# The first scan's sums turned on VectorE, loads ahead of stores on SyncE, and the variance of x half a step later

## Chip, cores and metric

One core of one Trainium2 chip. The metric is the device time of one execution in microseconds; the kernel before was run three times.

## What is computed

x is (16, 64, 128, 64) float32: 16 images of 64 rows, 128 columns and 64 channels. Two layers are added to it in turn; _gn is a normalisation over 32 groups of two channels each.

```python
def _L0_conv_ref(x, attention_centers, attention_spreads, token_proj_n_bias):
    ...
    posmap = jax.nn.softmax(pos_score, axis=1)
    xr = x.reshape(b, w, n, v, s)
    out = jnp.einsum('mns,bwnvs->bwmvs', posmap, xr)
    out = out + token_proj_n_bias[None, :, :, :, None]
    return out.reshape(b, w, n, c)

def _L1_conv_ref(x, W):
    rows = jnp.moveaxis(x, 1, 0)
    row0 = rows[0]
    def step(carry, row):
        new = row + jax.nn.relu(conv1d_same(carry, W))
        return (new, new)
    _, outs = jax.lax.scan(step, row0, rows[1:])
    out = jnp.concatenate([row0[None], outs], axis=0)
    return jnp.moveaxis(out, 0, 1)

x = x + _L0_conv_ref(_gn(x), ...)
x = x + _L1_conv_ref(_gn(x), L1_conv_W)
```

The first layer mixes each image's columns with four 128x128 matrices (one per head). The second runs down the 64 rows of an image: each new row is the normalised row plus the rectified convolution (9 taps along the columns, 64 by 64 channels) of the row before. That scan is sequential in the rows and independent between images.

## The kernel before

The 16 images go in two waves of eight. A setup phase (to about 180 us) prepares the first eight images. Then the first scan (wave 0) runs its 64 steps over these eight images, and beside it the other eight images are prepared, one per iteration of eight steps. A boundary follows, and then the second scan (wave 1) of 64 steps, with nothing beside it.

A step works in two halves s = 0, 1 of four images each. Data of the scan lie with (two columns' channels) on the 128 partitions and 256 elements (64 column pairs of four images) along each. For each half, in this order of dependence:

- PE, `convolve` (L1033): 15 matmuls into ps_conv; ten need carry_h (the high part of the row before, L1037) and the last five carry_l (its rest, L1041).
- VectorE, carry (L825): the rectified convolution plus the normalised row.
- ScalarE, carry_h (L543), rounded from carry; then VectorE, carry_l (L835), carry less carry_h.
- GpSimd, `add_carry` (L410): total, which is x after the first layer plus carry: a row of the output, still with the columns of an image scattered.

**From total to the output.** In wave 0, PE's `turn_out` (L1022) transposes total of both halves by four 128x128 matmuls against the identity into ps_out, right behind the step's first convolution; ScalarE's `stage_out` (L517) copies ps_out into one of two buffers `staged`; SyncE's `store_row` (L295) stores it with two DMAs of 128 KB in runs of 512 bytes. In wave 1, VectorE's `flip_out` (L804) transposes total in blocks of 32x32 straight into `staged`, behind the next step's carry of the same half; the rest of the turning is in the addresses of eight DMAs of 32 KB in runs of 128 bytes (`flipped_block`, L237), of which SyncE issues five (L306) and ScalarE three (L525). A buffer may be written again when its stores of two rows before have landed; GpSimd may write total again when it has been turned.

**Beside wave 0.** Each engine's `prep` function puts the next image's work into the steps by hand. The letter i is the step in an iteration, and VectorE counts four gaps in a step: gap 0 between carry and carry_l of half 0, gap 1 behind that carry_l, gaps 2 and 3 the same for half 1. Per iteration:

- GpSimd scales x by the first normalisation in eight halves of a quarter (`scale_half`, L379); PE mixes one in each step (`mix_half`, L949), at the end of the step; VectorE adds that to x in steps 1, 3, 5, 7, gap 3 (`mix_to_x1`, L732); PE turns it in steps 0, 2, 4, 6 (`turn_in`, L962); ScalarE keeps it (`keep_in`, L491) and normalises rows for the scan (L513).
- Statistics of the image after that (x of b + 1): 16 bn_stats on VectorE (L638), two or three each in gaps 0, 1, 2 of step 3, gaps 0, 2 of step 4 and gaps 0, 1 of step 5; PE averages them over the partitions at the end of step 5 (mean1, L965); VectorE's dev (step 5, gap 3), ScalarE's dev2 (end of step 5); PE's var1 (step 6, behind the first convolution, L969); ScalarE's root std1 (step 6, half 0); VectorE's guess1 (step 6, gap 2); ScalarE's square1 (end of step 6); VectorE's ratio1 and rstd1 (step 7, gap 0) and mean_rstd1 (step 7, gap 2); PE's shift1 (end of step 7, L974).
- Loads: SyncE issues four loads of 512 KB per iteration, in steps 1, 3, 5, 7, each behind that step's stores (L324 to L327). A load waits until PE has turned the quarter that the buffer held.

Each engine executes its own instructions in the order written; semaphores are the only links between engines.

## Time and profile before

| | us |
|---|---|
| runs | 787.57, 787.59, 785.27 (median 787.57) |
| profiled execution, its own time | 787.0 |
| its span | 785.2 |
| setup and first eight images | to about 183 |
| first scan | about 183 to 535 |
| boundary | about 535 to 552 |
| second scan | to the end |

Over the span PE is busy 703.5 us (90%), VectorE 580.8 (74%), ScalarE 524.2 (67%), GpSimd 421.0 (54%). Such a share is an average over stages with different limits; the page's strip of 40 slices shows PE at nine tenths or more in nearly every slice of both scans. How to read the rows further below: a row of a timeline is start, duration, engine, line, operation and tiles, with merged neighbours as "x2", and in brackets the idle time of that engine before it and what ended it. PE's weight loads (PEld) run beside its matmuls, whose recorded durations overlap, so the time that a piece of PE's work takes is read from start to start.

### The profile page before, as it was taken

Reading aid. Unit: us, or ns where it says so; the run is one execution under the profiler, and the core shown is the slowest. Engines: PE = TensorE matmul, PEld = TensorE weight load, DVE = VectorE, ACT = ScalarE, POOL = GpSimd, SP = SyncE. Lnnn points to the kernel's source line nnn. Section 1 sums busy time; section 2 is a strip of 40 time slices with the busy share of each in tenths; the row PEclk is TensorE's granted clock in tenths of the full one; section 3 lists DMA queues with packets and bytes.
Section 4 is the critical chain, followed back from the end, with each engine's and each line's share of the span. In section 5 each row is a group of like instructions: output and inputs, shape, how many; then the busy total and the mean of one; then the engine's idle time right before and its main releaser. Section 6 shows DMA issues by size and latency. Waiting matters only on the chain.

```text
span 785.2 us, 18039 instructions
## 1 busy us (share of the span) xinstructions
PE 703.5 (90%) x5356; PEld 671.4 (86%) x5356; DVE 580.8 (74%) x1298; ACT 524.2 (67%) x918; POOL 421.0 (54%) x416
## 2 busy tenths in 40 slices
PE   1577777767999999999999999995999999999996
PEld 1466666667999999999999999995999999999996
DVE  7589999955868787786868777664766767777775
ACT  1167767785877777777777777756566666666661
POOL 1555566623655556565656565661455555555553
PEclk9889999998999999999999999998999999999999
DMA  9846556132434443444434431221344444444444
GB/s 179 157 109 133 122 121 134 28 81 49 100 76 101 108 95 84 94 108 94 93 81 107 96 80 43 53 56 27 52 74 76 71 73 74 71 75 68 78 69 80
DMA packets 307594, 68.11 MB, mean 87 GB/s; under 512 B 274772, under 2 KB 307540, under 8 KB 307540
## 3 DMA queue, kind: packets, MB, share of 16 engines
q1 hardware_dynamic: 255316, 61.15, 38.0%
q10 hardware_dynamic: 52224, 6.30, 5.2%
q8 instruction: 26, 0.43, 0.2%
q14 instruction: 28, 0.23, 0.1%
HBM read 33.85 MB, written 33.55 MB: 86 GB/s over the span
## 4 chain that ended last, share of the span: by engine, by line
PE 58%; DVE 15%; issue 11%; ACT 7%; ACTq 6%; POOL 1%; SPq 0%; DVEq 0%; DMA 0%; POOLq 0%
PE ps_conv L1037 26%; PE ps_conv L1041 13%; PE ps_mix L949 9%; PE ps_in L962 6%; ACTq L533 5%; DVE st L638 5%; PE ps_out L1029 3%; ACT x_paired L491 2%; DVE carry L825 2%; ACT carry_h L543 2%; PE ps_small L939 2%; DVE x_sb L732 2%; DVE st L739 2%; ACT rows L513 1%; DVE rows L732 1%
## 5 line engine op out<-in xcount | busy, mean ns | idle before, releaser
L410 POOL TENSOR_TENSOR total<-x_paired,carry 128x256 f32<-128x256 f32 x256 | 234.2, 915 | 256.6 <-DVE carry L825 145.8
L835 DVE TENSOR_TENSOR carry_l<-carry,carry_h 128x256 fp32r<-128x256 f32 x252 | 166.1, 659 | 82.6 <-ACT carry_h L543 74.1
L543 ACT ACTIVATE carry_h<-carry 128x256 fp32r<-128x256 f32 x252 | 105.5, 419 | 162.9 <-DVE carry L825 115.8
L513 ACT ACTIVATE rows<-x_paired,shift,rstd 128x256 f32 (+1 forms) x256 | 213.4, 842 | 0.2
L1037 PE MATMUL ps_conv<-carry_h,wh 128*128 128x256 f32 x1280 | 208.1, 293 | 4.7 <-ACT carry_h L543 4.2
L491 ACT ACTIVATE x_paired<-ps_in,shift 64x512 f32<-64x512 f32 (+1 forms) x256 | 174.8, 683 | 30.2 <-PE ps_in L962 26.0
L1041 PE MATMUL ps_conv<-carry_l,wh 128*128 128x256 f32 x1280 | 194.6, 282 | 0.0
L1037 PE MATMUL ps_conv<-carry_h,wl 128*128 128x256 f32 x1280 | 193.9, 282 | 0.0
L1037 PEld LDWEIGHTS ps_conv<-carry_h,wh 128*128 128x128 f32 x1280 | 170.6, 191 | 8.1 <-ACT carry_h L543 6.9
L379 POOL TENSOR_TENSOR xs<-x_sb,minus_rstd 128x512 f32<-128x512 f32 x104 | 147.9, 1435 | 43.8 <-DVE minus_rstd L714 40.9
L1037 PEld LDWEIGHTS ps_conv<-carry_h,wl 128*128 128x128 f32 x1280 | 171.0, 189 | 0.0
L1041 PEld LDWEIGHTS ps_conv<-carry_l,wh 128*128 128x128 f32 x1280 | 171.0, 189 | 0.0
L825 DVE SCALAR_TENSOR_TENSOR carry<-ps_conv,rows 128x256 f32<-128x256 f32 x256 | 106.6, 417 | 72.9 <-PE ps_conv L1041 62.7
L949 PE MATMUL ps_mix<-xs,mix 128*128 128x256 f32 x384 | 102.2, 397 | 0.0
L739 DVE BATCH_NORM_STATS2 st<-x_paired 128x6 f32<-128x512 f32 (+1 forms) x128 | 85.4, 681 | 8.9 <-ACT x_paired L491 8.9
L949 PEld LDWEIGHTS ps_mix<-xs,mix 128*128 128x128 f32 x384 | 70.6, 199 | 7.2
L638 DVE BATCH_NORM_STATS2 st<-x_sb 128x6 f32<-128x256 f32 x208 | 75.0, 412 | 0.0
L962 PE MATMUL ps_in<-ident,x_sb 128*128 128x128 f32 x416 | 55.4, 277 | 15.5 <-ACT x_paired L491 11.3
L962 PEld LDWEIGHTS ps_in<-ident,x_sb 128*128 128x128 f32 x416 | 48.0, 143 | 22.7 <-issue 19.0
L812 DVE STREAM_TRANSPOSE staged<-total 128x256 f32<-128x256 f32 x128 | 55.4, 433 | 3.6 <-DMA out_dram<-staged 3.4
L732 DVE SCALAR_TENSOR_TENSOR x_sb<-ps_mix,bias_col,x_sb 128x1024 f32<-128x1024 f32 x42 | 53.5, 1274 | 3.2 <-PE ps_mix L949 3.2
L379 POOL TENSOR_TENSOR xs<-rows,minus_rstd 128x512 f32<-128x512 f32 x24 | 31.3, 1334 | 32.7 <-DVE minus_rstd L714 31.2
(92 smaller groups left out, 396.7 us busy)
## 6 DMA issues: line engine op xcount, KB each, us to landing
x_sb<-in_x_dram SPq DMA_DIRECT2D x52, 512.0 KB, 4.2
out_dram<-staged SPq DMA_DIRECT2D x128, 128.0 KB, 2.4
out_dram<-staged SPq DMA_DIRECT2D x320, 32.0 KB, 1.6
rows<-in_x_dram SPq DMA_DIRECT2D x12, 512.0 KB, 4.1
out_dram<-staged ACTq DMA_DIRECT2D x192, 32.0 KB, 1.7
x_paired<-in_L_conv_W_dram SPq DMA_DIRECT2D x2, 80.0 KB, 2.7
x_paired<-in_L_conv_W_dram SPq DMA_DIRECT2D x2, 64.0 KB, 2.5
x_paired<-v_attention_centers_dram SPq DMA_DIRECT2D x1, 0.0 KB
```

Of the source, the lines that this page charges most:

```text
L379: nc.gpsimd.tensor_tensor(xs[:, c % 2, heads, :, :].rearrange("p s h v -> p h v s"), src, minus_rstd1[:, k, m:G:2].unsqueeze(1).unsqueeze( ...
L410: nc.gpsimd.tensor_tensor(total[s][:, :].rearrange("p (w j) -> p w j", w=WS), x1_rows(wave, it, i, 1, s * WS, WS)[:, 0, :, :], carry[s][:, ...
L491: ins = nc.scalar.activation(dst[q * C:(q + 1) * C, r:CR:2, :], src[:, q, :, :], ACT.Identity, bias=shift1[r * C:(r + 1) * C, k:k + 1])
L513: nc.scalar.activation(rows[:, g % 2, :, w // WS, :, w % WS], x1_rows(wave, it, g * RG, RG, w, 1)[:, :, 0, :], ACT.Identity, scale=rstd2[: ...
L543: nc.scalar.activation(carry_h[s][:, EDGE:EDGE + J, :].rearrange("p j w -> p (j w)"), carry[s][:, :], ACT.Copy).then_inc(high_ready[s], 1)
L638: ins = nc.vector.bn_stats(st1[:, 0, 2 * m:2 * m + 2, :].rearrange("p g k -> p (g k)"), v[:, m, :, :, :])
L825: nc.vector.scalar_tensor_tensor(carry[s][:, :], ps_conv[:, s * BANK:s * BANK + SW], 0.0, rows[:, (i // RG) % 2, i % RG, s, :, :].rearrang ...
L835: nc.vector.tensor_tensor(carry_l[s][:, EDGE:EDGE + J, :].rearrange("p j w -> p (j w)"), carry[s][:, :], carry_h[s][:, EDGE:EDGE + J, :].r ...
L949: ins = nc.tensor.matmul(ps[:, s * CR * V:(s + 1) * CR * V], mix[:, s, :], xs[:, c % 2, s, :, :].rearrange("p h v -> p (h v)"), start=True ...
L962: ins = nc.tensor.transpose(ps_in[:, k * P:(k + 1) * P], x_bufs[e][:, at:at + P], ident[:, :])
L1037: nc.tensor.matmul(ps_conv[:, s * BANK:s * BANK + SW], w[:, d, :], carry_h[s][:, d:d + J, :].rearrange("p j w -> p (j w)"), start=(w is wh ...
L1041: ins = nc.tensor.matmul(ps_conv[:, s * BANK:s * BANK + SW], wh[:, d, :], carry_l[s][:, d:d + J, :].rearrange("p j w -> p (j w)"), start=F ...
```

## The change

VectorE's flips, so far in the second scan alone, now turn the first scan's sums too: `flip_out` runs behind carry in both waves, and twice more behind the last step of wave 0. `turn_out`, `stage_out` and `store_row` are gone, with ps_out's use for rows. GpSimd's add waits for the flip of its half. SyncE stores each row of wave 0 with eight DMAs of 32 KB, all on its own queue (in wave 1 still five, with three on ScalarE's), and in each step it now issues the load, if there is one, ahead of the row's stores. The variance of x is worked out half a step later: PE's var1 behind the mix of step 6 in place of behind its first convolution, ScalarE's std1 in half 1 of step 6 and square1 in half 0 of step 7, VectorE's guess1 in gap 0 of step 7 and ratio1 and rstd1 in gap 2, ahead of mean_rstd1.

```diff
@@ sync
             def store_flipped(wave, h, buf):
-                rows_flipped = held(sp, h + 1)
+                rows_flipped = held(sp, wave * H + h + 1)
                 alone(sp, w_zeroed)
                 for s in range(NS):
                     sp.wait_ge(out_flipped[s], rows_flipped)
-                for block in range(SP_BLOCKS):
+                for block in range(BLOCKS if wave == 0 else SP_BLOCKS):
                     dst, src = flipped_block(wave, h, buf, block)
                     sp.dma_start(dst, src).then_inc(flip_stored[buf], 16)
...
-                    if wave == 1 and not (is_zero(it) and i == 0):
-                        store_flipped(wave, it * STEPS + i - 1, (i + 1) % 2)
-                    if wave == 0 and not (is_zero(it) and i == 0):
-                        store_row(wave, it * STEPS + i - 1, (it + wave * ITERS) * STEPS + i, (i + 1) % 2)
                     if i == 1 and more >= 1:
                         load_chunk(b + 1, 1 - e, CH - 1, CH * b)
                     if i in (3, 5, 7) and more >= 2:
                         load_chunk(b + 2, e, (i - 3) // 2, CH * b + (i - 3) // 2 + 1)
+                    if not (is_zero(it) and i == 0):
+                        store_flipped(wave, it * STEPS + i - 1, (i + 1) % 2)
@@ gpsimd, add_carry
-                if wave == 0 and not is_zero(t):
-                    pool.wait_ge(out_turned, t)
...
+                if not is_zero(t):
+                    pool.wait_ge(out_flipped[s], t)
@@ scalar, iteration
-                        if s == 0 and wave == 0 and not begins:
-                            stage_out(t, (i + 1) % 2)
...
-                        if s == 0 and i == 6 and more:
+                        if s == 1 and i == 6 and more:
                             std1_of(b + 1)
+                        if s == 0 and i == 7 and more:
+                            square1_of(b + 1)
...
-                    if i == 6 and more:
-                        square1_of(b + 1)
@@ vector, prep
-                    if i == 6 and gap == 2:
+                    if i == 7 and gap == 0:
                         guess1_of(b + 1)
-                    if i == 7 and gap == 0:
+                    if i == 7 and gap == 2:
                         ratio1_of(b + 1)
                         rstd1_of(b + 1, 1 - e)
-                    if i == 7 and gap == 2:
                         mean_rstd1(b + 1, 1 - e)
@@ vector, flip_out
-                if isinstance(h, int) and h < 2:
-                    dve.wait_ge(stored[buf], H // 2 * 32)
-                else:
-                    dve.wait_ge(flip_stored[buf], 128 * (it * (STEPS // 2) + (i - 1) // 2))
+                if not (wave == 0 and isinstance(h, int) and h < 2):
+                    dve.wait_ge(flip_stored[buf], 128 * (wave * H // 2 + it * (STEPS // 2) + (i - 1) // 2))
@@ vector, iteration, and behind the last step of wave 0
-                        if wave == 1 and not (is_zero(it) and i == 0):
+                        if not (is_zero(it) and i == 0):
                             flip_out(wave, it, i, s)
...
+            for s in range(NS):
+                dve.wait_ge(total_ready[s], H)
+                flip_out(0, ITERS, 0, s)
             finish(B - 1, 1)
@@ tensor, prep and iteration
-                if after == 0:
-                    if i == 6 and more:
-                        var1_of(b + 1, inv_p[:, :], 1)
-                else:
+                if after == 1:
                     mix_half(b, i // 2, i % 2, ps_mix, b * CH + i // 2)
                     if i == 0 and prev:
                         turn_in(b - 1, 1 - e, CH - 1)
+                    if i == 6 and more:
+                        var1_of(b + 1, inv_p[:, :], 1)
...
-                            if s == 0 and wave == 0:
-                                turn_out(t)
```

## Rows read from the trace of the kernel before

**Rows 1.** Busy us (instructions) by engine in a stretch; then granted clock, DMA share, GB/s.

```profile
core 0: us, PE busy (x) PEld busy (x) DVE busy (x) ACT busy (x) POOL busy (x), PEclk, DMA share, GB/s
302.00:346.00 44.00, 43.78 (x348) 42.29 (x347) 34.08 (x69) 33.82 (x61) 25.75 (x26) 1.00 0.42 95
```

**Rows 2.** Chain of waits, 300 to 560: start us, duration us, what.

```profile
343.93 0.74 DVE st L638 x2
...
433.15 0.74 DVE st L638 x2
```

**Rows 3.** Timeline, PE: transposes between convolutions, and convolutions of the second scan.

```profile
353.72 0.60 PE L1029 MATMUL ps_out<-ident,total 128*128 128x128 f32 x4
354.08 0.83 PE L1037 MATMUL ps_conv<-carry_h,wh 128*128 128x256 f32 x5
...
355.92 1.03 PE L949 MATMUL ps_mix<-xs,mix 128*128 128x256 f32 x4
...
603.05 0.75 PE L1037 MATMUL ps_conv<-carry_h,wh 128*128 128x256 f32 x5
...
604.82 0.75 PE L1037 MATMUL ps_conv<-carry_h,wh 128*128 128x256 f32 x5
```

**Rows 4.** Timeline of a half step of the second scan; the flip's line (min/median/max ns).

```profile
601.47 0.42 DVE L825 SCALAR_TENSOR_TENSOR carry<-ps_conv,rows 128x256 f32<-128x256 f32 x1
...
601.81 0.43 DVE L812 STREAM_TRANSPOSE staged<-total 128x256 f32<-128x256 f32 x1
...
602.38 0.43 DVE L835 TENSOR_TENSOR carry_l<-carry,carry_h 128x256 fp32r<-128x256 f32 x1
...
602.48 1.05 POOL L410 TENSOR_TENSOR total<-x_paired,carry 128x256 f32<-128x256 f32 x1 [0.18 <-DVE staged L812]
...
L812 DVE STREAM_TRANSPOSE staged<-total x128: 427/433/448, 552.5 to 779.5; 128x256 f32<-128x256 f32 x128
```

**Rows 5.** Groups by line, VectorE, 302 to 346 and 560 to 780: busy, mean | idle before.

```profile
L835 DVE TENSOR_TENSOR carry_l<-carry,carry_h 128x256 fp32r<-128x256 f32 x16 | 12.6, 787 | 4.5 <-ACT carry_h L543 4.5
...
L835 DVE TENSOR_TENSOR carry_l<-carry,carry_h 128x256 fp32r<-128x256 f32 x120 | 67.5, 563 | 43.1 <-ACT carry_h L543 35.0
```

**Rows 6.** Timeline of steps 3 to 5: first carry, VectorE's idle time, PE's mean1.

```profile
330.98 0.42 DVE L825 SCALAR_TENSOR_TENSOR carry<-ps_conv,rows 128x256 f32<-128x256 f32 x1 [0.43 <-PE ps_conv L1041]
...
342.21 0.42 DVE L825 SCALAR_TENSOR_TENSOR carry<-ps_conv,rows 128x256 f32<-128x256 f32 x1 [1.19 <-PE ps_conv L1041]
...
345.09 0.31 PE L939 MATMUL ps_small<-st,inv_p 128*128 128x32 f32 x2
```

**Rows 7.** Timeline: POOL's add begun before carry_l.

```profile
345.17 0.87 POOL L410 TENSOR_TENSOR total<-x_paired,carry 128x256 f32<-128x256 f32 x1 [1.45 <-DVE carry L825]
...
345.48 0.84 DVE L835 TENSOR_TENSOR carry_l<-carry,carry_h 128x256 fp32r<-128x256 f32 x1 [0.48 <-ACT carry_h L543]
```

**Rows 8.** Timeline: var1 on PE; ratio, rstd, product with the mean; shift1 on PE.

```profile
347.90 0.30 PEld L939 LDWEIGHTS ps_small<-st,inv_p 128*128 128x128 f32 x2 [0.45 <-ACT dev L454]
...
354.26 0.19 DVE L707 SCALAR_TENSOR_TENSOR ps_small<-ps_small,square 128x32 f32<-128x32 f32 x1
354.57 0.19 DVE L714 SCALAR_TENSOR_TENSOR minus_rstd<-ps_small,guess 128x32 f32<-128x32 f32 x1
...
356.46 0.28 DVE L719 TENSOR_TENSOR minus_mean_rstd<-ps_small,minus_rstd 128x128 f32<-128x128 f32 x1
...
356.80 0.30 PEld L939 LDWEIGHTS ps_small<-col_avg,minus_mean_rstd 128*128 128x128 f32 x2 [0.25 <-DVE minus_mean_rstd L719]
```

**Rows 9.** Timeline, ScalarE at the boundary: the last copy from ps_out.

```profile
539.37 0.60 ACT L523 ACTIVATE staged<-ps_out 128x512 f32<-128x512 f32 x1
```

**Rows 10.** Stores on SyncE's queue (ns to issue), and DMA issues (KB, us to landing).

```profile
L314 SPq DMA_DIRECT2D out_dram<-staged x320: 315/316/2336, 555.2 to 783.1; - x160
...
L303 SPq DMA_DIRECT2D out_dram<-staged x128: 595/607/1723, 189.4 to 540.7; - x128
...
x_sb<-in_x_dram SPq DMA_DIRECT2D x52, 512.0 KB, 4.2
...
out_dram<-staged SPq DMA_DIRECT2D x320, 32.0 KB, 1.6
```

More of the change, by code:

```diff
@@ L200, in mix_and_scan_kernel @@
         total_ready = [sem(f"total_ready{s}") for s in range(NS)]
-        out_turned = sem("out_turned")
-        out_staged = sem("out_staged")
-        stored = [sem(f"stored{n}") for n in range(2)]
         out_flipped = [sem(f"out_flipped{s}") for s in range(NS)]
@@ L293, in _ @@
                 load_chunk(W + 1, 1, c, CH * (W - 1) + c + 1)
-            def store_row(wave, h, t, buf):
-                staged_rows = held(sp, t)
-                alone(sp, w_zeroed)
-                sp.wait_ge(out_staged, staged_rows)
-                src = staged[:, buf, :].rearrange("p (m f) -> p m f", f=P)
-                for e in range(2):
-                    dst = out_pairs[wave * W + e:(wave + 1) * W:2, bass.ds(h, 1), :, :]
-                    sp.dma_start(dst.rearrange("m h j f -> (h j) m f"),
-                                 src[e * J:(e + 1) * J, :, :]).then_inc(stored[buf], 16)
             def store_flipped(wave, h, buf):
-                rows_flipped = held(sp, h + 1)
+                rows_flipped = held(sp, wave * H + h + 1)
                 alone(sp, w_zeroed)
@@ L557, in iteration @@
                     if wave == 1 and not begins:
-                        store_flipped(1, it * STEPS + i - 1, (i + 1) % 2)
+                        store_flipped(wave, it * STEPS + i - 1, (i + 1) % 2)
                     if b is not None:
@@ L828, in iteration @@
                             ALU.max, ALU.add).then_inc(carry_ready[s], 1)
-                        if wave == 1 and not (is_zero(it) and i == 0):
+                        if not (is_zero(it) and i == 0):
                             flip_out(wave, it, i, s)
@@ L1020, in finish @@
                 var2_of(b, wave)
-            def turn_out(t):
-                if not (isinstance(t, int) and t <= 1):
-                    pe.wait_ge(out_staged, t - 1)
-                for s in range(NS):
-                    pe.wait_ge(total_ready[s], t)
-                    for m in range(WS // 2):
-                        ins = nc.tensor.transpose(ps_out[:, s * SW + m * P:s * SW + (m + 1) * P],
-                                                  total[s][:, m * P:(m + 1) * P], ident[:, :])
-                ins.then_inc(out_turned, 1)
             def convolve(t, s):
```

18 lines of the change are left out of this document (3 added, 15 removed).

## The prediction

> **What bounds the kernel now.** I read the busy times by stretch first, then the chain of waits through the same stretch, then the timeline of one iteration. One iteration of the first scan (eight steps, one image prepared beside them) takes 44.6 us (343.93 to 433.15, two of them [rows 2]); the stretch 302 to 346 is nearly all of one, and in it PE is busy 43.78 of 44.00 us, VectorE 34.08, ScalarE 33.82 and POOL 25.75, with the granted clock at 1.00, so at the higher of its two levels, 2.4 GHz [rows 1]. What leaves PE's queue here is time gained, until something else ends last. The chain names the candidate: although PE is so full, the chain leaves it once per iteration, in step 5, for VectorE's statistics of x [rows 2]. VectorE is close to being the bound in a few steps long before it is one on average.
>
> **What leaves PE.** In every step but the first, four transposes stand between the step's two convolutions. They start at 353.72, the next convolution at 354.08 (0.36 us), and that convolution takes 1.84 us to the mix behind it; in the second scan, where a convolution follows another directly, it takes 1.77 (603.05 to 604.82) [rows 3]. So the transposes cost 0.36 + 0.07 = 0.43 us. 63 steps have them: 27.1 us less, 3.4 us per iteration. The 64th set, after the last step, lies beside VectorE's last mix_to_x1, which the turning of the image waits for: nothing. ScalarE loses 64 copies of 0.60 us; it has idle time in every step, so only the one at the scans' boundary counts, where it stands ahead of seven row normalisations in a row that ScalarE does back to back [rows 9]: 0.6 us less.
>
> **What VectorE gains in work.** 126 transposes move from the nearest row's form, the flips of the second scan: 0.433 us each, hardly varying [rows 4]. There carry lasts 0.42 but the flip starts 0.34 after it, so an instruction gives way some 0.08 before its recorded end; I take 0.35 per flip. In most half steps this is free: carry_l waits for ScalarE's carry_h anyway and starts 0.91 after carry with the flip in between (601.47 to 602.38) [rows 4], and before, the wait in that place was 4.5 us in this stretch [rows 5].
>
> It isn't free in steps 3 to 5, where bn_stats fill the gaps. PE's average of these statistics (mean1, in step 5, 7 iterations) stands behind the last of them. Before, counted from carry of step 3 at 330.98: the last pair of statistics begins at 343.93 and ends at 344.67 [rows 2], so 13.69 us, of which VectorE idled 1.19 (ahead of 342.21); PE came for them at 345.09, 14.11 us after the same start, so nothing waited [rows 6]. After: VectorE runs without idling, 13.69 - 1.19 + 5 flips x 0.35 = 14.25, with 0.06 to reach PE 14.31 (0.06 as from 356.74, the end of minus_mean_rstd, to 356.80 [rows 8]). PE is there after 14.11 - 3 x 0.43 = 12.82. PE waits 1.5 us: 10.5 us over 7 iterations. Later mixes and convolutions that would have waited for a late VectorE (carry_h, or POOL's scaled halves behind the later adds) have these 1.5 us too, so I add nothing for them.
>
> Bounds: carry_l lasts 0.84 where POOL's add began first (345.17 against 345.48) and 0.43 where carry_l did (602.38 against 602.48) [rows 4, 7]. If the three long ones of this run become short, 3 x 0.41 = 1.2 less: 0.3 us wait. If the flips take all of 0.433 (+0.4) and two more carry_l become long (+0.8): 2.7. I take 1.5, since statistics still stand ahead of carry_l in those steps and the add, 0.67 behind the flip's start, gets ahead of it.
>
> **POOL.** Its add waited for carry and for PE's transposes; now it waits for the flip, and starts 0.67 after the flip's start [rows 4], so about a flip later than carry alone would let it. Behind the add stand the next add and a scaled half for the coming mix. POOL is busy 25.75 of 44.00 us [rows 1], so 0.4 us later is covered except where VectorE is already late, and there mean1 is waited for longer.
>
> **The variance, half a step later.** Six instructions move: PE's var1 behind the mix, ScalarE's root and square, VectorE's guess, ratio and rstd. Gained: PE's wait for ScalarE's dev in front of var1, 0.45 us in 7 iterations [rows 8]; the mix, recorded with 1.03 [rows 3], now covers it: 3.1 us. Lost: ratio, rstd and the product with the mean now all stand in the last half step, behind carry and flip, and PE's shift1 waits for the product. Before, the product stood right behind carry, so 0.34 after its start, and PE waited 0.25 for it (356.80). After: 0.34 + flip 0.35 + ratio to rstd 0.31 (354.26, 354.57) + 0.31 of the same kind = 1.31, so 0.97 later, all of it PE's wait, since PE already waited: 6.8 us [rows 8]. Bounds: 0.6 if the flip's wait is shared, 1.4 if a long carry_l precedes it. On ScalarE the root waits in a later place with keep_in and the next carry_h behind it, a step of slack; POOL's first scaled half waits for rstd no longer than for its own add.
>
> **SyncE's queue.** Eight stores of 32 KB for two of 128 KB: 0.316 to issue each, landing 1.6 later [rows 10], so 8 x 0.32 = 2.5 us of a 5.3 us step, with a load on odd steps. The load now waits for in_turned ahead of the eight stores; that comes from PE in the step before, and the stores wait for flips of this step, so the wait is over first. The flip two rows on waits for the stores: 8.4 us after the row's last flip (below), against 2.5 + 1.6. Behind a flip that waits stand carry_l, the gap's work and the next carry, so PE would follow. I take nothing. Bounds: no gain, since nothing waited for stores before; a loss only under the last rival.
>
> **Sum.** Against the profiled execution's 787.0 (span 785.2 and 1.8 around it; median of runs 787.57, so 0.6 higher): -27.1 + 10.5 + 6.8 - 3.1 - 0.6 = -13.5, so 773.5. With the lower bounds of both waits, -27.1 + 2.1 + 4.2 - 3.1 - 0.6 = -24.5: 762.5. With the upper ones, -27.1 + 18.9 + 9.8 - 3.1 - 0.6 = -2.1: 785.
>
> **Rivals.** (1) VectorE fits: short carry_l almost everywhere, both waits near their lower bounds, 763. For it: the second scan's order, carry, flip, carry_l, is now the first's. Against: there no statistics stand in the gaps.
>
> (2) Both waits near the upper bounds: 785, hardly a gain.
>
> (3) Slower: VectorE bounds the whole wave. Its place is carry_l behind POOL's add in every half step, which the flip starts: add 0.67 after the flip's start, 0.87 long, carry_l's end 0.28 after that (345.17 + 0.87 to 345.48 + 0.84) [rows 4, 7]. A half step then takes 0.34 + 1.82 - 0.08 = 2.08, sixteen 33.3; of VectorE's other work, 34.1 less carry (16 x 0.34) and carry_l (16 x 0.71, its mean of 0.79 less 0.08 [rows 5]) = 17.3, the 16 statistics (0.66 a pair, 5.3) fit into that wait, so 45.3, and 0.6 for ratio and rstd: 45.9 against 44.6. Over 7 iterations 9.1 more: 796. It decides from the point where carry_h comes later than the add, 0.67 after the flip. For it: in the second scan carry_l wins by 0.10 only (602.38 against 602.48). Against it: it does win there mostly, with a mean of 0.563 [rows 5], and the scan isn't bound by it. By the Trainium skill ("VectorE: DVE Perf Modes", Rules for kernel authors) 128x128 transposes belong on TensorE where PSUM will do, the 32x32 ones on VectorE; by the first half of it this move costs. No row shows it as a rule: here TensorE is the full engine.
>
> (4) The stores land late: if each took 0.607 to issue, as the 128 KB one [rows 10], behind a load of 4.2 us, 4.9 + 4.2 + 1.6 = 10.7 us pass the 8.4 that two buffers give (two steps of 5.3 less a convolution and a flip), 2.3 us on 4 rows of each iteration, 74 us in all: near 847. It decides from 0.32 each with the load right ahead. Against it: the same store took 0.316 (median of 320), and SyncE issues the load once the row before is out, 5.3 - 2.5 us ahead of the flips. The Trainium skill ("DMA: Bandwidth & Descriptors", Specifications) wants 512 B per transfer, below which it expects read-modify-write; these write 128 B runs, and the second scan, which does too, lets VectorE run on.
>
> **How the numbers follow.** Forecast 0.53, (1) 0.15, (2) 0.17, (3) 0.12, (4) 0.03. The range 762 to 786 holds the first three. 0.3% is 2.4 us, about what a measurement tells from no change; faster takes the forecast, (1) and 0.10 of (2): 0.78; same 0.07 of (2); slower (3) and (4): 0.15.
>
> **What would show it.** In the profile after: PE without L1029; a first-scan iteration of 43.2 us (44.6 - 3.4 + 1.5 + 0.97 - 0.45); PE idle ahead of mean1 on VectorE's statistics, 1.5 us, 7 times, and ahead of shift1 on minus_mean_rstd, 1.2 us; none ahead of var1; flips at 0.43 with no wait for stores. Wrong if the two waits aren't there (then nearer 763), if convolutions wait for carry_h or carry_l in steps 0 to 2 (then 796), or if flips wait for stores.

## The result, and the profile of the kernel after

The kernel after takes 775.16 us (median; 774.53 to 779.17), the kernel before 786.42 in the same comparison: a ratio of 0.9867, 95% interval 0.983 to 0.990. So it is 11.3 us faster where 13.5 were forecast, and 775.2 lies 1.7 above the forecast of 773.5. The profiled execution of the kernel after took 779.17, with a span of 777.4; it is the slowest of them.

The page's line of busy times after, over the whole span:

```profile
PE 682.4 (88%) x5100; PEld 645.6 (83%) x5100; DVE 592.8 (76%) x1426; ACT 490.2 (63%) x854; POOL 431.0 (55%) x416
```

PE works 21 us less than before (703.5), ScalarE 34 less (524.2). VectorE works 12 more (580.8), though its new flips take 55. The groups of carry_l in the first scan tell why (busy, mean | idle before), after and before:

```profile
L799 DVE TENSOR_TENSOR carry_l<-carry,carry_h 128x256 fp32r<-128x256 f32 x124 | 63.8, 514 | 10.9 <-ACT carry_h L513 2.2
```

```profile
L835 DVE TENSOR_TENSOR carry_l<-carry,carry_h 128x256 fp32r<-128x256 f32 x123 | 92.1, 749 | 36.5 <-ACT carry_h L543 36.4
```

The flip fills VectorE's wait for carry_h, 36.5 us that are down to 10.9, and since GpSimd's add now starts behind the flip, carry_l mostly starts ahead of the add (31 of 126 take over 0.65 us, 109 before) and is 28 us shorter in all: so most of the flips' time is paid for in the place where they stand.

Where the span got shorter is to be seen in the time from one carry to another. The first carry of every iteration of eight steps stands in the timeline, here of iterations 5 and 6:

```profile
356.21 0.42 DVE L789 SCALAR_TENSOR_TENSOR carry<-ps_conv,rows 128x256 f32<-128x256 f32 x1 [0.97 <-PE ps_conv L996]
...
401.23 0.42 DVE L789 SCALAR_TENSOR_TENSOR carry<-ps_conv,rows 128x256 f32<-128x256 f32 x1 [0.60 <-PE ps_conv L996]
```

Their differences, in both kernels, are the seven iterations with an image prepared beside them:

| first-scan iteration | 1 | 2 | 3 | 4 | 5 | 6 | 7 | sum |
|---|---|---|---|---|---|---|---|---|
| before, us | 42.55 | 44.57 | 44.50 | 44.72 | 44.51 | 44.34 | 44.40 | 309.6 |
| after, us | 41.78 | 42.68 | 42.93 | 43.28 | 45.02 | 42.83 | 42.56 | 301.1 |

The forecast was 43.2 for each. Iterations 2, 3, 6 and 7 are a little better than that, iteration 4 is at it, and iteration 5 is 1.8 us worse and even longer than before. The ledger of the two profiled executions, from the same carries:

| stretch | before | after | difference |
|---|---|---|---|
| start to the first carry of the first scan | 183.2 | 185.5 | +2.3 |
| seven iterations | 309.6 | 301.1 | -8.5 |
| eighth iteration and the boundary | 54.8 | 50.2 | -4.6 |
| second scan, first to last carry | 230.0 | 233.0 | +2.9 |
| behind the last carry | 7.6 | 7.6 | 0 |

The two lines of the first scan hold the change's own work: -13.1 for -13.5 forecast. The setup has no changed instruction, and its end moves from one profiled execution to the next (181.0 in the fastest kernel below, 183.3 in another). The granted clock up to there moves with it: 0.94 here, 0.96 before, 0.98 and 0.96 in those two. So +2.3 belongs to this execution; without it the ledger gives -10.2, near the 11.3 of the medians. The +2.9 of the second scan was not forecast.

The two waits that the prediction put a price on are both there. The waits of the first scan after (us in total, times, longest):

```profile
PEld ps_small L906 <- DVE minus_mean_rstd L686: 7.5, 7, 1.1
PE ps_small L906 <- DVE st L605: 7.3, 7, 1.1
PEld ps_small L906 <- DVE st L605: 7.2, 5, 1.5
DVE staged L776 <- DMA out_dram<-staged: 3.4, 2, 1.8
PEld ps_small L906 <- issue: 2.9, 2, 1.4
```

and the same view of before:

```profile
PEld ps_small L939 <- ACT dev L454: 2.9, 7, 0.5
PEld ps_small L939 <- DVE minus_mean_rstd L719: 1.8, 7, 0.3
```

PE's weight load is what waits first, so its rows carry the price. For mean1 (on VectorE's statistics, st) it waits 7.2 us in five iterations, and in the other two the same wait of 1.4 is put down to "issue", with the matmul behind it still naming st: 10.1 us in seven, for 10.5 forecast. For shift1 (on minus_mean_rstd) it waits 7.5 for 1.8 before: 5.7 more, for 6.8. The wait ahead of var1 (on dev), 2.9 before, is gone, for 3.1. One row was forecast not to be there: flips wait for their buffer's stores, 3.4 us.

The chain of mean1, from the timeline of steps 4 to 6 of one iteration:

```profile
416.04 0.42 DVE L789 SCALAR_TENSOR_TENSOR carry<-ps_conv,rows 128x256 f32<-128x256 f32 x1 [1.02 <-PE ps_conv L996]
...
417.05 0.87 POOL L388 TENSOR_TENSOR total<-x_paired,carry 128x256 f32<-128x256 f32 x1 [1.09 <-DVE staged L776]
417.36 0.84 DVE L799 TENSOR_TENSOR carry_l<-carry,carry_h 128x256 fp32r<-128x256 f32 x1
...
429.66 0.74 DVE L605 BATCH_NORM_STATS2 st<-x_sb 128x6 f32<-128x256 f32 x2
430.46 0.30 PEld L906 LDWEIGHTS ps_small<-st,inv_p 128*128 128x128 f32 x2 [1.47 <-DVE st L605]
```

From carry of step 3 to PE's mean1 it is 430.46 - 416.04 = 14.42, for 14.31 forecast, and PE's wait is 1.47 for 1.5. The add at 417.05 starts ahead of carry_l at 417.36, which then takes 0.84: the long carry_l that the prediction left in these steps, 0.28 past the add's end.

The chain of shift1, in the last half step of an iteration:

```profile
351.90 0.42 DVE L789 SCALAR_TENSOR_TENSOR carry<-ps_conv,rows 128x256 f32<-128x256 f32 x1 [0.44 <-PE ps_conv L996]
352.25 0.43 DVE L776 STREAM_TRANSPOSE staged<-total 128x256 f32<-128x256 f32 x1
352.60 0.17 DVE L674 SCALAR_TENSOR_TENSOR ps_small<-ps_small,square 128x32 f32<-128x32 f32 x1
352.89 0.19 DVE L681 SCALAR_TENSOR_TENSOR minus_rstd<-ps_small,guess 128x32 f32<-128x32 f32 x1
353.12 0.29 DVE L686 TENSOR_TENSOR minus_mean_rstd<-ps_small,minus_rstd 128x128 f32<-128x128 f32 x1
353.46 0.30 PEld L906 LDWEIGHTS ps_small<-col_avg,minus_mean_rstd 128*128 128x128 f32 x2 [1.14 <-DVE minus_mean_rstd L686]
```

The product starts 1.22 after carry, for 1.31 forecast (rstd to product took 0.23, not 0.31), and PE waits 1.14. One flip costs VectorE 0.35 here (352.25 to 352.60), as taken.

### What the long steps of iteration 5 wait for

SyncE's queue holds the answer. Its stores and loads around them, from the timeline (merged neighbours as x16; the lengths of a merged row hold the gaps between its stores):

```profile
343.01 2.75 SPq L299 DMA_DIRECT2D out_dram<-staged  x1
...
358.65 0.81 SPq L299 DMA_DIRECT2D out_dram<-staged  x2
...
362.64 0.89 SPq L299 DMA_DIRECT2D out_dram<-staged  x2
...
366.87 0.42 SPq L267 DMA_DIRECT2D x_sb<-in_x_dram  x1
367.61 8.72 SPq L299 DMA_DIRECT2D out_dram<-staged  x16
```

and the whole line of the stores, with what SyncE does between two of them (min/median/max ns):

```profile
L299 SPq DMA_DIRECT2D out_dram<-staged x832: 315/316/2752, 193.0 to 775.3; - x167
L299 SPq FUSED_REGOPS  x536: 37/37/66, 272.7 to 772.7; - x179
```

A store is still recorded with 0.316 here, but stores follow each other at 0.50 us (two at 358.65 take 0.81 = 0.50 + 0.31), so that eight are 4.0 us, not 2.5. From 272.7 on the program runs in a loop and works its addresses out in registers, and a register operation and a move stand between two stores; they don't make the pace, though. Ahead of the loop and behind it nothing stands between two stores of a row, one from the second on is recorded with 0.45, and the next begins 0.49 after its start. A row of eight takes as long in the loop (first line) as behind it (second):

```profile
283.12 3.81 SPq L299 DMA_DIRECT2D out_dram<-staged  x8
...
504.24 3.78 SPq L299 DMA_DIRECT2D out_dram<-staged  x8
```

The kernel before had this pace too, in the five stores of a row of its second scan (2.31 = 4 x 0.50 + 0.31):

```profile
613.74 2.31 SPq L314 DMA_DIRECT2D out_dram<-staged  x5
```

The first store right behind a load takes longer, 0.7 to 1.2 us in twelve of thirteen places (1.09 at 367.61) and 2.75 in the other; 14 of the first scan's other 499 stores took 0.8 to 1.7 as well. And at the loop's end SyncE issues nothing from 359.46 to 362.64: 0.12 behind the last store stands its jump, 2.74 us pass from that to the next instruction, and the flips of the row that it goes on with had ended at 358.82. The same jump takes 0.33 in the kernel before and 0.19 in the run without flips (below), where a pass of SyncE's loop has 170 and 42 instructions; in every run whose pass has 362 or 458 it takes 2.5 to 2.8, in one 3.7. An estimate from these rows: 16 rows at 4.15, 8 loads at 1.4 with what the store behind them loses, and the jump make 80 us of the 86 that 16 steps of 5.35 have. The queue is all but full.

The flips that waited, both of them in iteration 5 (VectorE):

```profile
367.73 0.45 DVE L776 STREAM_TRANSPOSE staged<-total 128x256 f32<-128x256 f32 x1 [1.59 <-DMA out_dram<-staged]
...
373.45 0.45 DVE L776 STREAM_TRANSPOSE staged<-total 128x256 f32<-128x256 f32 x1 [1.77 <-DMA out_dram<-staged]
```

The row issued from 362.64 on goes out until 366.5 and has landed at 367.7, where the first flip starts. The next row is issued from 367.61, behind a load, with a first store of 1.09, and lands at about 373.4. Had the first row been issued 2.7 us earlier, as its flips allowed, it would have landed at about 365.0, ahead of 366.14, where VectorE came for the buffer, and the next one at about 370.7, ahead of 371.68. But the jump alone doesn't do it: SyncE came to it late. The store of 2.75 us at 343.01 had put it behind, and the last row ahead of the jump went out from 354.86, 2.2 us after its flips (352.68). In the run with the variance back (below), whose queue is the same, SyncE issued that row 0.2 after its flips; its jump took 2.54, the next row went out 1.7 after its flips, no flip waited, and iteration 5 took 43.71, the one before it 43.95. So in this execution the long store, the jump and the pace of 0.50 together made the two waits, and the steps of 5.60 and 7.95 us (5.27 and 6.15 in the iteration before). No run took the jump away, and why it takes 2.74 no row shows.

### The profile page after: what moved, and what is told of

Read it like the earlier page. It is cut to its first block, busy times and chain, and to the rows that moved or that the text cites. A ratio compares the mean times of both kernels' runs of the same rounds, so it can differ in the third digit from the quotient of the medians.

```text
span 777.4 us, 18263 instructions
## 1 busy us (share of the span) xinstructions
PE 682.4 (88%) x5100; PEld 645.6 (83%) x5100; DVE 592.8 (76%) x1426; ACT 490.2 (63%) x854; POOL 431.0 (55%) x416
## 4 chain that ended last, share of the span: by engine, by line
PE 46%; DVE 23%; issue 13%; ACTq 6%; ACT 6%; SPq 3%; POOL 1%; DVEq 1%; DMA 0%; POOLq 0%
PE ps_conv L992 22%; PE ps_conv L996 11%; DVE st L605 7%; PE ps_mix L916 7%; ACTq L503 6%; PE ps_in L929 5%; DVE carry L789 3%; DVE st L706 3%; SPq L299 3%; DVE carry_l L799 2%; ACT carry_h L513 2%; DVE staged L776 2%; PE ps_small L906 2%; ACT x_paired L469 2%; DVE x_sb L699 2%
## 5 line engine op out<-in xcount | busy, mean ns | idle before, releaser
L388 POOL TENSOR_TENSOR total<-x_paired,carry 128x256 f32<-128x256 f32 x256 | 252.2, 985 | 237.8 <-DVE staged L776 230.6
L992 PE MATMUL ps_conv<-carry_h,wh 128*128 128x256 f32 x1280 | 204.7, 291 | 6.7 <-ACT carry_h L513 6.3
L799 DVE TENSOR_TENSOR carry_l<-carry,carry_h 128x256 fp32r<-128x256 f32 x252 | 134.6, 534 | 58.9 <-ACT carry_h L513 41.9
L361 POOL TENSOR_TENSOR xs<-x_sb,minus_rstd 128x512 f32<-128x512 f32 x104 | 139.8, 1356 | 45.7 <-DVE minus_rstd L681 34.1
L776 DVE STREAM_TRANSPOSE staged<-total 128x256 f32<-128x256 f32 x256 | 110.7, 433 | 5.4 <-DMA out_dram<-staged 5.0
L916 PE MATMUL ps_mix<-xs,mix 128*128 128x256 f32 x384 | 105.3, 407 | 0.6 <-DVE x_sb L699 0.4
```

The lines of the kernel that those rows point to most:

```text
L361: nc.gpsimd.tensor_tensor(xs[:, c % 2, heads, :, :].rearrange("p s h v -> p h v s"), src, minus_rstd1[:, k, m:G:2].unsqueeze(1).unsqueeze( ...
L388: nc.gpsimd.tensor_tensor(total[s][:, :].rearrange("p (w j) -> p w j", w=WS), x1_rows(wave, it, i, 1, s * WS, WS)[:, 0, :, :], carry[s][:, ...
L776: nc.vector.transpose(staged[:, buf, s * SW:(s + 1) * SW], total[s][:, :]).then_inc(out_flipped[s], 1)
L799: nc.vector.tensor_tensor(carry_l[s][:, EDGE:EDGE + J, :].rearrange("p j w -> p (j w)"), carry[s][:, :], carry_h[s][:, EDGE:EDGE + J, :].r ...
L916: ins = nc.tensor.matmul(ps[:, s * CR * V:(s + 1) * CR * V], mix[:, s, :], xs[:, c % 2, s, :, :].rearrange("p h v -> p (h v)"), start=True ...
L992: nc.tensor.matmul(ps_conv[:, s * BANK:s * BANK + SW], w[:, d, :], carry_h[s][:, d:d + J, :].rearrange("p j w -> p (j w)"), start=(w is wh ...
```

## Experiments

Each run stands against the kernel before on the same chip (787 to 788 us). Line numbers in rows are those of the kernel that ran. First, the transposes alone.

**No flips in the first scan**

```diff
-                if not (is_zero(it) and i == 0):
+                if wave == 1 and not (is_zero(it) and i == 0):
                     flip_out(wave, it, i, s)
...
             def store_flipped(wave, h, buf):
+                if wave == 0:
+                    return
```

(The waits that count flips and stores change with it.)

> The changed kernel without the first scan's turning and without its stores, but for the last row's flip (the first eight images are not written). Theory A (PE's transposes cost 0.43 us each, and VectorE's flips give 1.5 us per iteration back in PE's wait for mean1): an iteration of 44.6 - 3.4 - 0.45 + 0.6 = 41.3 us, no wait ahead of mean1, 786.4 - 27.1 - 3.1 + 4.3 - 0.6 = 760 us. Rival R1 (the transposes cost PE less than that, and nothing is given back): the iteration stays at the changed kernel's 42.7 and the time near 774.

Measured: 760.48 us, ratio 0.967 (0.964 to 0.970); iterations 2 to 7 of 40.9 to 41.4 us, 41.3 expected. What the transposes on PE cost is thereby gained in full where nothing takes their place, and the 15 us between this run and the kernel after are what the flips and their stores give back. The waits of its first scan:

```profile
PEld ps_small L908 <- DVE minus_mean_rstd L688: 5.2, 7, 0.8
```

mean1's wait is down to 1.3 us in five iterations; shift1's falls to 5.2 but stays, since the moved ratio and rstd make it too.

**Four statistics fewer, so that the last ones end in step 4** (the last four of 16 are left out)

```diff
-                    if i == 5 and gap < 2:
-                        stats1(b + 1, 1 - e, 12 + 2 * gap, 2)
```

> The changed kernel without the four statistics instructions of step 5 (two gaps of two; their groups keep the image before's values). Theory A (PE's mean1 waits for VectorE's run from step 3 to the last statistics): the run is 4 x 0.33 = 1.3 us shorter and ends a carry_l earlier, PE waits for nothing there, 1.4 us less per iteration, 7 iterations, 775.2 - 10 = 765. Rival R2 (what waits next is nearly as late: the mix waits for GpSimd's scaled half behind the flips, or a convolution for carry_h): 2 us less, 773, with PE's wait moved there.

Measured: 766.62 us, ratio 0.976 (0.972 to 0.980); iterations 40.81, 41.40, 41.57, 42.47, 43.74, 41.47, 41.25. The waits of its first scan:

```profile
PEld ps_small L904 <- DVE minus_mean_rstd L686: 7.5, 7, 1.1
DVE staged L774 <- DMA out_dram<-staged: 5.1, 6, 1.7
```

PE no longer waits for statistics, and the time falls by 8.5, near the 10.1 of that wait. The rest went to the buffers: flips wait 5.1 us for stores, 3.4 in the kernel after. A PE that comes round sooner meets the same store queue.

**The same with all the work in it: statistics from step 2 on.** Gap 3 of step 2 takes three of them, and step 5 keeps one.

```diff
+                    if i == 2 and gap == 3:
+                        stats1(b + 1, 1 - e, 0, 3)
...
-                        stats1(b + 1, 1 - e, 2 * gap, 2)
+                        stats1(b + 1, 1 - e, 3 + 2 * gap, 2)
...
-                        stats1(b + 1, 1 - e, 6 + 3 * gap // 2, 3)
-                    if i == 5 and gap < 2:
-                        stats1(b + 1, 1 - e, 12 + 2 * gap, 2)
+                        stats1(b + 1, 1 - e, 9 + 3 * gap // 2, 3)
+                    if i == 5 and gap == 0:
+                        stats1(b + 1, 1 - e, 15, 1)
```

> The changed kernel with its 16 statistics begun earlier: three at the end of step 2, where VectorE idles 1.0 us, six in step 3, six in step 4, one in step 5. Nothing is left out. Theory A: VectorE's run from step 3 to the last statistics is 3 x 0.33 + the carry_l and two statistics behind it shorter, 12.6 against PE's 12.8, no wait ahead of mean1: 1.4 us less per iteration, 775.2 - 10 = 765.5. Rival R2 (the work only moves, and the next late thing is nearly as late): 773.

Measured: 768.19 us, ratio 0.977 (0.975 to 0.980), 2.7 above the expectation; iterations 41.02, 41.47, 43.08, 42.57, 43.92, 41.50, 41.26. Outside iterations 3 to 5 they are those of the run before. In 3 to 5 flips wait:

```profile
DVE staged L778 <- DMA out_dram<-staged: 7.0, 8, 1.8
```

**The variance moved back, the flips kept**

```diff
@@ scalar, iteration
-                        if s == 1 and i == 6 and more:
+                        if s == 0 and i == 6 and more:
                             std1_of(b + 1)
-                        if s == 0 and i == 7 and more:
-                            square1_of(b + 1)
...
+                    if i == 6 and more:
+                        square1_of(b + 1)
@@ vector, prep
+                    if i == 6 and gap == 2:
+                        guess1_of(b + 1)
                     if i == 7 and gap == 0:
-                        guess1_of(b + 1)
-                    if i == 7 and gap == 2:
                         ratio1_of(b + 1)
                         rstd1_of(b + 1, 1 - e)
+                    if i == 7 and gap == 2:
                         mean_rstd1(b + 1, 1 - e)
@@ tensor, prep
-                if after == 1:
+                if after == 0:
+                    if i == 6 and more:
+                        var1_of(b + 1, inv_p[:, :], 1)
+                else:
...
-                    if i == 6 and more:
-                        var1_of(b + 1, inv_p[:, :], 1)
```

> The changed kernel with the variance of x in its old places. Theory A (the move pays together with the flips): VectorE's dev and ScalarE's dev2 come some 1.0 us after PE has reached the old place of var1, so PE waits about 1.1 there; ahead of shift1 it waits 0.6 less. 0.5 more per iteration, 775.2 + 3.5 = 779. Rival R3 (the move only adds a wait, ahead of shift1): 0.5 less per iteration, 772.

**The variance moved alone, in the kernel before** (the same lines the other way)

> The kernel before with the variance's move alone. Theory A: var1's wait of 0.45 goes, the product comes 0.6 later behind ratio and rstd and PE waits for it: 0.2 more per iteration, 786.4 + 1 = 787.5, not told from no change. Rival R5 (the move is worth something by itself): 0.45 less per iteration with the product's delay covered, 783.

Measured: moved back 779.78 us, ratio 0.992 (0.990 to 0.995), so 4.6 slower than the kernel after. Moved alone 785.24, ratio 0.998 (0.997 to 1.000): a gain of 1.3 us by the ratio, 2.6 at most by its interval, between the two expectations, and its iterations are those of before (44.58, 44.42, 44.74, 44.42 in the middle). The rows that tell why, first with the variance back:

```profile
PEld ps_small L907 <- ACT dev L432: 7.8, 7, 1.1
...
PEld ps_small L907 <- DVE minus_mean_rstd L686: 5.1, 7, 1.0
```

then with it moved alone:

```profile
PEld ps_small L938 <- DVE minus_mean_rstd L719: 5.2, 7, 0.8
```

Without flips the move takes var1's wait away (2.9) and raises shift1's from 1.8 to 5.2: nothing is left of it. With flips var1's wait would have been 7.8 and shift1's 5.1 in any case; the move trades 7.8 for 2.4. So it pays only together with the flips. In an iteration of the run with the variance back, var1 waits for ScalarE's part of dev:

```profile
433.24 0.23 ACT L432 ACTIVATE dev<-dev 128x32 f32<-128x32 f32 x1
```

VectorE's part was done at 431.63, but ScalarE was at its keep_in (431.83 to 433.21), which stands behind a carry_h that VectorE's run of statistics and flips had made late. It starts 2.9 us after PE's mean1, 2.5 in the kernel before, and PE, with no transposes between, comes to var1 2.0 after mean1, 2.4 before.

**Ratio and rstd out of shift1's chain.** In step 7 guess1 (half 0) and the product (half 1) go ahead of the flip, ratio and rstd into the gap between, and ScalarE's square1 ahead of its row normalisation.

```diff
@@ scalar, iteration
+                        if s == 0 and i == 7 and more:
+                            square1_of(b + 1)
...
-                        if s == 0 and i == 7 and more:
-                            square1_of(b + 1)
@@ vector, iteration
+                        if b is not None and more and i == 7:
+                            if s == 0:
+                                guess1_of(b + 1)
+                            else:
+                                mean_rstd1(b + 1, 1 - e)
                         if not (is_zero(it) and i == 0):
                             flip_out(wave, it, i, s)
@@ vector, prep
-                    if i == 7 and gap == 0:
-                        guess1_of(b + 1)
-                    if i == 7 and gap == 2:
+                    if i == 7 and gap == 1:
                         ratio1_of(b + 1)
                         rstd1_of(b + 1, 1 - e)
-                        mean_rstd1(b + 1, 1 - e)
```

> The changed kernel with the variance's last links shortened: in step 7 guess and the product with the mean stand ahead of the flip, ratio and rstd one gap earlier, ScalarE's square ahead of its row normalisation. Theory A: the product begins 0.34 after carry in place of 1.22, PE's wait ahead of shift1 falls from 1.1 to 0.25, 0.85 less per iteration, 775.2 - 6 = 769. Rival R6 (PE then waits for something else there, carry_l or the mix): 774.

Measured: 770.95 us, ratio 0.980 (0.978 to 0.982); 769 expected of a wait that bounds, 774 of one that is hidden. The wait is back at the value of before, and 4.2 us of its 5.7 show up in the time (6.1 in the seven iterations of the two profiled executions, 1.4 of them in iteration 5):

```profile
PEld ps_small L908 <- DVE minus_mean_rstd L686: 1.8, 7, 0.3
```

**Both waits taken away** (early statistics and the short chain together)

> The two edits together (statistics begun in step 2, and the shortened links). Theory A: both waits are separate, so the gains add: 775.2 - 10 - 6 = 759.5, an iteration of 40.4 us, near what PE's own work takes. Rival R2 with R6: 770 or more.

Measured: 765.68 us, ratio 0.974 (0.972 to 0.977); iterations 40.00, 40.67, 42.91, 42.39, 43.49, 40.64, 40.49. Four of them are at the expected 40.4. The other three are among the four that run in SyncE's loop, and there flips wait for stores:

```profile
DVE staged L775 <- DMA out_dram<-staged: 8.2, 10, 2.1
```

In the run without flips, which has no stores in that scan, these three take 41.0, 41.4 and 41.0. So the gains add up until flips wait for the store queue, and stop there. This is read from the waits; the run that was to free the queue (two stores on ScalarE, below) put another wait in the place, so no run shows what the queue alone is worth.

**Stores ahead of the load again**

```diff
+                    if not (is_zero(it) and i == 0):
+                        store_flipped(wave, it * STEPS + i - 1, (i + 1) % 2)
                     if i == 1 and more >= 1:
                         load_chunk(b + 1, 1 - e, CH - 1, CH * b)
                     if i in (3, 5, 7) and more >= 2:
                         load_chunk(b + 2, e, (i - 3) // 2, CH * b + (i - 3) // 2 + 1)
-                    if not (is_zero(it) and i == 0):
-                        store_flipped(wave, it * STEPS + i - 1, (i + 1) % 2)
```

> The changed kernel with each row's stores ahead of the load, as before. Theory A (SyncE's order is hidden either way): 775 within 2 us, an iteration of 42.7. Rival R4 (a load ahead of the eight stores blocks the queue, and flips wait for stores): 2 to 3 us less, no wait of a flip for stores.

Measured: 782.08 us, ratio 0.9935 (0.992 to 0.995): 7 slower than the kernel after, and neither expectation (775 and 772) held. Its waits and SyncE's queue:

```profile
DVE st L605 <- DMA x_sb<-in_x_dram: 8.5, 7, 2.9
```

```profile
317.14 9.91 SPq L299 DMA_DIRECT2D out_dram<-staged  x16
327.36 0.41 SPq L267 DMA_DIRECT2D x_sb<-in_x_dram  x1
```

The load can go only when eight stores are through, and those wait for a flip of the same step, so x comes late and VectorE's statistics stand, 8.5 us in seven iterations. I had looked at the order for what it does to the stores; its worth is what it does for the load.

**Two of eight stores on ScalarE's queue in the first scan**, in the kernel after and in the one with both waits taken away. The expectations count iterations from 0, so their 2 to 5 are 3 to 6 here. Their 0.35 us outside the loop is wrong: it is the time behind a row's first store alone, and from the second on it is 0.49 (above).

```diff
-    SP_BLOCKS = 5
+    SP_BLOCKS = [6, 5]
...
-                    if wave == 1 and not begins:
+                    if not begins:
                         # ScalarE's stores of the row before, blocks SP_BLOCKS[wave] to 7
```

> The changed kernel with six of the first scan's eight stores on SyncE's queue and two on ScalarE's. In the profile after, SyncE issues one store every 0.50 us inside its loop (iterations 2 to 5; 0.35 outside), so 4.0 us a step plus the load, and iterations 2 to 4 take 42.9, 43.3 and 45.0 us against 42.6 to 42.8 of the others, with flips that wait for stores. Theory S (SyncE's queue is nearly full in its loop, and what it falls behind comes back as flips that wait): 3.0 us a step, no flip waits for stores, iterations 2 to 5 at 42.6, 3 us less: 772. Rival T (those iterations are longer for another reason, or ScalarE's issues delay its carry_h as much): 775 or more, the iterations as uneven.

> The kernel with statistics begun in step 2 and the shortened links (765.7), with the same split of the stores. There iterations 0, 1, 5 and 6 take 40.0 to 40.7 us and iterations 2 to 4 42.4 to 43.5. Theory S (the two gains did not add because SyncE's queue is the next bound): iterations 2 to 5 at 40.6, 765.7 - 7 = 759. Rival T: 765 or more.

Measured: 776.04 us (774.78 to 779.63), ratio 0.986 (0.982 to 0.990), no gain over the kernel after; and 772.68, ratio 0.981 (0.978 to 0.984), 7 us worse than the run with both waits gone. The flips' waits for stores are gone from the first scan. In their place, in the first of the two:

```profile
DVE carry_l L799 <- ACT carry_h L513: 14.1, 27, 1.3
ACT x_paired L469 <- issue: 13.3, 34, 3.4
```

In the second they are 19.7 and 15.2. ScalarE has carry_h on the path of every half step; two issues on its queue, with their gaps, delay that, and carry_l and PE behind it (2.2 us for carry_l in the kernel after). In the second shift1's wait comes back too, 8.0 us for 2.9.

**The reverse for the second scan: two stores on ScalarE in place of three**, first on top of the last run

```diff
-    SP_BLOCKS = [6, 5]
+    SP_BLOCKS = [6, 6]
```

> The same with six and two in the second scan too (five and three so far). Theory U (in the second scan a convolution waits for carry_h behind ScalarE's three issues): one issue of 0.45 us less in that place, a step of 3.55 to 3.6 in place of 3.64, 3 to 5 us less than the kernel with the split in the first scan alone. Rival V (something else sets that step, or SyncE's six at 0.50 us are late): no change or slower by 2.

Measured: 766.74 us, ratio 0.975 (0.972 to 0.978), 5.9 less than the run before it; an iteration of the second scan takes 28.32 for 29.2.

**Early statistics, short chain, all the first scan's stores on SyncE, two of the second's on ScalarE**

```diff
-    SP_BLOCKS = 5
+    SP_BLOCKS = 6
```

> Statistics begun in step 2, the shortened links, all eight stores of the first scan on SyncE again, and the second scan's split at six and two. Theory U with A: the second scan's iterations at 28.3 us in place of 29.15, 7 x 0.85 = 6 less than the kernel with the two edits (765.7): 759.5. Theory S's remainder stays: iterations 2 to 4 of the first scan 2 to 3 us longer than the others. Rival: SyncE, now issuing six in both, is late in the second scan after the first, and the gain is half: 763.

Measured: 759.2 us (755.93 to 763.18), ratio 0.963 (0.959 to 0.968), as expected: 27 to 29 us faster than the kernel before and 16 faster than the kernel after. First-scan iterations 40.79, 41.04, 41.30, 43.22, 44.15, 40.64, 40.55, second-scan 28.32. What is left stands in these rows, its flips' wait in the first scan and the longest of them:

```profile
DVE staged L775 <- DMA out_dram<-staged: 7.7, 8, 2.9
```

```profile
360.20 0.45 DVE L775 STREAM_TRANSPOSE staged<-total 128x256 f32<-128x256 f32 x1 [2.94 <-DMA out_dram<-staged]
```

Here too it follows the loop's jump (at 351.96, 2.79 us to the next instruction), to which SyncE came 2.3 us late.

What the third store does in the second scan is to be seen in ScalarE's queue. The kernel after:

```profile
658.62 1.39 ACTq L503 DMA_DIRECT2D out_dram<-staged  x3
...
659.19 0.42 DVE L789 SCALAR_TENSOR_TENSOR carry<-ps_conv,rows 128x256 f32<-128x256 f32 x1 [0.27 <-PE ps_conv L996]
...
660.11 0.42 ACT L513 ACTIVATE carry_h<-carry 128x256 fp32r<-128x256 f32 x1 [0.91 <-DVE staged L776]
```

and the last kernel:

```profile
643.69 0.89 ACTq L503 DMA_DIRECT2D out_dram<-staged  x2
644.43 0.42 DVE L788 SCALAR_TENSOR_TENSOR carry<-ps_conv,rows 128x256 f32<-128x256 f32 x1 [0.43 <-PE ps_conv L1000]
...
644.89 0.42 ACT L513 ACTIVATE carry_h<-carry 128x256 fp32r<-128x256 f32 x1 [0.61 <-DVE carry L788]
```

With three stores carry_h starts 0.92 after carry, behind the issues; with two, 0.46. The profile names the flip as what ended the wait, but that flip began at 659.53 and none of these rows needed it: the three stores, which stand ahead of carry_h in ScalarE's order and wait for flips, had theirs when the first was issued at 658.62.

## Why the prediction was right, and where not

**The transposes (-27.1).** Right, and shown by the run without flips: 41.3 expected, 40.9 to 41.4 measured. The Trainium skill ("VectorE: DVE Perf Modes", Rules for kernel authors) sends 128x128 transposes to TensorE; by it the move costs, and the measurement decides otherwise here, where TensorE was the full engine [rows 1]: 0.987.

**mean1's wait (+10.5).** Right: 10.1, in the place, by the chain and with the long carry_l that were forecast. That it bounds is shown by the two runs that shorten the statistics (8.5 and 7.0 us less).

**shift1's wait (+6.8) and var1's (-3.1).** The sums are near (5.7 and 2.9). The step rstd to product was sized 0.08 too long, which is half of the 1.1 by which shift1's wait is smaller. The two were told as a cost of moving the variance, 3.7 net; the runs turn that round. Against before the move alone is worth about nothing, and beside the flips it saves 4.6, because they would have made var1 wait 7.8. The prediction compared each edit with the kernel before, not with the other edits in place, so its sum held while its shares did not.

**The boundary (-0.6).** Too small: the step from the last row of the first scan to the first of the second takes 15.19 for 16.65, so -1.5. What else moved there was not tried; the granted clock in it was 0.95 for 0.85.

**SyncE's queue (nothing).** This is the step that failed. Its 8 x 0.32 took the time that a store's issue is recorded with for the time from one to the next. That is 0.50, and the first store behind a load and the loop's jump come on top; the rows that I had read [rows 10] hold lengths and no gaps, while the second scan before, from which they are, has the 0.50 (the five stores above). The price in the profiled execution is 3.4 us of flips' waits in one iteration, and 2.3 of its time (iteration 5 against 42.7 for the others). Iteration 4 is 0.6 longer than those without such a wait, and is the longest before and in the run without flips too (44.72, 41.38). Rival (4) had the mechanism, with too high a price per store (0.607) and a load that holds the queue for its 4.2 us; here a load costs some 1.4 by the estimate above, and the waits come at the jump, with a queue that was late before it. And the load's new place, costed at nothing, is what the queue can't do without: 7 us. That the first scan came within 0.4 us of its forecast (-13.1 for -13.5) is in part luck: the queue's 2.3 are made up for by shift1's smaller wait (1.1) and by the boundary (0.9).

The Trainium skill ("DMA: Bandwidth & Descriptors", Specifications) wants 512 bytes or more per transfer; these stores of 128-byte runs landed 1.6 us after issue (median of the line), as in the second scan before [rows 10]. What made rows late was their issue.

**The second scan (not forecast).** From the third on its iterations take 29.14 to 29.20 for 28.80 to 28.87, 1.9 us of the 2.9 with the last one, with no instruction of it moved. The first iteration has the other 1.1, 31.0 for 29.9; it takes 29.3 to 31.1 in the runs, at a granted clock of 0.89 to 0.93. The longer later ones are found in every run with SP_BLOCKS 5 in the second scan whose counts of flips and stores run on from the first scan (29.1 to 29.3), and in none whose counts begin with that scan (before, the variance moved alone, no flips: 28.8 to 28.95). Part of ScalarE's register operations there take longer (57 ns for 51, 60 for 46), and it issues its first store 258 ns behind the flip for 245. That these few ns, on a ScalarE whose third store already delays carry_h, make the 0.04 us per step is argued, not shown; with two stores the steps are at 3.54 us with the same counts, which fits.

**Rivals.** That VectorE fits (763) falls by the two waits. That VectorE bounds the wave (796) falls by the iterations with both waits gone, 40.5 with all 16 flips in place, and by carry_l's mean of 514 ns. The large waits (785) did not come.

**What stays open.** The store of 2.75 us at 343.01: no run tells its cause. What fills the 2.74 us of the jump. The cause of the second scan's 0.04 us per step.

## To carry to other kernels

Size a queue by the time from one issue to the next, not by the recorded length of one, and count its loop's jump and the extra of an issue behind a large transfer: here 0.32 us recorded stood for 0.50, and a queue that looked half empty was full. Price an edit with the other edits in place as well as alone; a move that is worth nothing by itself was worth 4.6 us beside the flips. An engine with a link of the chain in every step, as ScalarE here, should issue as few DMAs as the others can take over, and the load whose data are due goes ahead of the stores.

## What the runs showed of the hardware that I had not expected

- SyncE issues a 32 KB store every 0.49 to 0.50 us, whether it is recorded with 0.316 (in a loop, with a register operation and a move ahead of each) or with 0.45 (in straight code); the first one right behind a 512 KB load took 0.7 to 1.2 in twelve of thirteen places, once 2.75.
- The jump at the end of the first scan's loop on SyncE took 2.74 us (2.5 to 2.8 in nine other runs, 3.7 in one), in which nothing was issued, where a pass of the loop has 362 or 458 instructions, and 0.2 to 0.3 where it has 42 or 170. Why is open.
- With three stores on ScalarE's queue per row the second scan's iteration is 29.15, with two 28.32, though SyncE then issues six for five.
- A transfer of work to VectorE made another of its instructions shorter: carry_l from a mean of 749 ns to 514, since the add that it collides with now comes behind it.
